# Another order of the rounding steps within a batch row of a conditional MoE and LoRA kernel

## The chip, the cores and the metric

One core of a Trainium2 chip runs the whole kernel. The metric is the device time of one execution in microseconds; lower is better. TensorE (PE) multiplies, VectorE (DVE), ScalarE (ACT) and GpSimd (POOL) do elementwise work, SyncE (SP) issues the DMAs. Each of them has its own queue of instructions, and semaphores tie the queues together.

## The reference

Eight batch rows of `x`, each 512 x 256, go through a mixture of experts with a residual, and then through a linear layer with a LoRA part and a residual. A row has its own two experts of eight, picked by `cond_8`, and one expert shared by all rows.

```python
# layer 0, for each batch row
w, sel = top_k(softmax(cond_8), 2); w = w / w.sum()
mlp(x, g, u, d) = (gelu(x @ g) * (x @ u)) @ d          # g, u: 256 x 1024, d: 1024 x 256
x = x + sum(w[e] * mlp(x, skill_gate[e], skill_up[e], skill_down[e]) for e in sel) \
      + mlp(x, shared_gate, shared_up, shared_down)
# layer 1
out  = einsum('btc,oc->bto', x, W_base) + b_base
h    = einsum('btc,erc->bter', x, As)                  # 8 adapters of rank 16
lora = einsum('bter,eor,be->bto', h, Bs, cond_8)
x = x + out + lora * 2.0
```

## The kernel before

**Numbers.** All matmuls are fp32 in three passes. Every operand is rounded to a short format (ACT, `take_hi`, written "hi") and its remainder is kept too (DVE, `take_lo`: operand minus hi, written "lo"); a product is hi x hi + hi x lo + lo x hi. Rounding and remainder together are called a split. So each weight and each activation passes ACT, then DVE, before TensorE may use it.

**Stages.** First the shared expert is done for all rows (until about 259 us), its result kept in DRAM. Then come the eight batch rows, called row 0 to row 7 here: row 0 is written out, rows 1 to 6 are a loop of three turns with two rows each, row 7 is written out. This change touches only the rows. A row takes some 68 us.

**Steps of a row.** A row has 16 steps, `k` = 0 to 15, one for each 128 of the 1024 hidden columns of its first and then of its second expert. Two steps share a pair of weights: pair 0 to pair 7 of a row, which lie in slot `pair % 4` of `raw` (raw weights, loaded by SP; slots 0 and 1 are called `raw`, 2 and 3 `xbuf`) and of `wide` (the split weights). In step `k` TensorE multiplies gate and up for `k` (into `ring`, 12 matmuls of 512 columns) and then down for step `k - 2` (into `ps_acc`, 6 matmuls). ACT takes the gelu, DVE multiplies gelu, up and the expert's weight (L1711), ACT rounds the product (`inner_hi`), DVE takes its remainder (`inner_lo`).

**Seven-product pairs.** Pairs 3, 5 and 7 (`SEVEN`) do both steps at once, at `k` = 6, 10 and 14, in seven block products instead of eight: 42 matmuls of 256 columns. They need sums of blocks of the weights (POOL makes them, `sums_of_weights`; ACT and DVE split them, `split_sums_w`) and sums of blocks of x (`split_sums_x`). The results come out of PSUM by two ACT copies (L1292) and DVE additions: `ex_v` at L1660, for which the seventh product waits, then L1662, L1669, L1671. Behind the 42 come the downs of the two steps before, into `ps_acc`.

**What else lies in a row.** Step 1: DVE adds up the previous row's result (`layer1_sum`, L1629) and it is split. Step 3: TensorE runs the previous row's second layer (`layer1`, 12 matmuls, `ps_acc`). Step 4: ACT adds the bias (`add_bias`, L1253), DVE transposes the output in blocks (`turn_output`, L1639). Step 8: LoRA's B, scaled by the row's `cond`, is split (`BW_STEP`, L1358 and L1726). Step 9: TensorE folds A and B (`fold`) and the next row's x is split (`X_STEP - 1`). Step 12: DVE adds the folded weights to W, `w_eff` (L1746); step 13: that is split. Row 0 alone has constants at step 4 (`CONST_STEP`): TensorE transposes W and B, ACT and DVE split A, DVE copies and adds the identity (`layer1_constants`, L1615 to L1620).

**What sets the order.** Nothing but the order in which each engine's part is written: ACT and DVE have the same loop over `k`, and two tables say at which step they split which pair and which sums:

```python
SPLIT_AT = {0: 2, 2: 3, 5: 4, 6: 5, 9: 6, 10: 7, 13: 8, 14: 9}
SUMS_AT = {2 * pr - 2: n_s for n_s, pr in enumerate(SEVEN)}
```

Pairs 8 and 9 are the next row's pairs 0 and 1, and the sums stand at steps 4, 8 and 12. A split of a pair waits until SP's load has landed and until TensorE is done with the old weights in that slot of `wide`; DVE's half waits for ACT's. TensorE asks for pair `p` at step `2p` (`weights_ready`), and SP loads a slot again when the pair in it is split.

Of the kernel before, what the change touches and what calls it, by code (L numbers as in the profile page):

```python
# [35 lines left out]
def cond_resid_kernel(nc, x, cond, skill_gate, skill_up, skill_down, shared_gate, shared_up,  # L36
# [15 lines left out]
    L1_STEP = 3  # L52
    CONST_STEP = 4
    BW_STEP = 8
# [3 lines left out]
    X_STEP = 10  # L58
# [6 lines left out]
    with ExitStack() as ctx:  # L65
# [317 lines left out]
        SPLIT_AT = {0: 2, 2: 3, 5: 4, 6: 5, 9: 6, 10: 7, 13: 8, 14: 9}  # L383
        SUMS_AT = {2 * pr - 2: n_s for n_s, pr in enumerate(SEVEN)}
# [675 lines left out]
        def _(act):  # L1060
# [251 lines left out]
            def row(b, par, first, last):  # L1312
                def split_pair(k):
                    pr = SPLIT_AT[k]
                    if pr >= 2 * PAIRS:
                        if not last:
                            split_routed(b + 1, 0, pr - 2 * PAIRS, down_done, b * K + 2 * pr - 6)
                    elif pr >= PAIRS:
                        split_routed(b, 1, pr - PAIRS, down_done, b * K + 2 * pr - 6)
                    elif first:  # L1320
                        split_routed(b, 0, pr, product_done, products(NU - PAIRS + pr, UP, NP - 1))
                    else:
                        split_routed(b, 0, pr, down_done, b * K + 2 * pr - 6)

                for k in range(K):
                    if k // 2 in SEVEN:
                        if k % 2 == 0:
                            n_s = SEVEN.index(k // 2)
                            ex_copy_out(b, n_s, first)
                            split_pair(k)  # L1330
# [12 lines left out]

                    if k == W_EFF_STEP + 1:
                        act.wait_ge(w_eff_done, b + 1)
                        take_hi(w_eff_s[0], w_eff[:]).then_inc(w_eff_hi, 1)
                    if k == (4 if first else 3):
                        split_sums_x(b, first)
                    if k in SUMS_AT:
                        split_sums_w(b, SUMS_AT[k])  # L1350
                    if k in SPLIT_AT:
                        split_pair(k)
# [13 lines left out]
                    if k == 1 and not first:  # L1366
                        layer1_hi(b - 1)
                    if k == L1_STEP + 1 and not first:
# [6 lines left out]
                    if k == X_STEP - 1 and not last:  # L1375
# [15 lines left out]
        def _(dve):  # L1391
# [292 lines left out]
            def row(b, par, first, last):  # L1684
                def split_pair(k):
                    pr = SPLIT_AT[k]
# [5 lines left out]
                for k in range(K):  # L1692
                    s = k // IC
                    if k // 2 in SEVEN:
                        if k % 2 == 0:
                            ex_seven(b, par, k, SEVEN.index(k // 2))
                            split_pair(k)
# [22 lines left out]
                    if k in SUMS_AT:  # L1720
                        split_sums_w(b, SUMS_AT[k])
                    if k in SPLIT_AT:
                        split_pair(k)
# [10 lines left out]
                    if first and k == 1:  # L1734
                        acc1_to_stage(Q - 1)
                    if k == L1_STEP + 1 and not first:
# [3 lines left out]
                    if k == X_STEP - 1 and not last:  # L1740
# [68 lines left out]
```

## Time and profile before

| | us |
|---|---|
| median of 3 runs | 804.69 (803.77 to 805.49) |
| profiled execution | 805.0 |
| its span, first to last instruction | 803.2 |
| granted TensorE clock in it | 0.999 |

| engine | busy share of the span |
|---|---|
| PE | 99% |
| DVE | 84% |
| ACT | 59% |
| POOL | 34% |

Read it so: times are counted from the first instruction. A line like `378.56 0.88 PE L733 MATMUL ps_ring<-... x6` is six matmuls written at line 733 that begin at 378.56 and of which the last ends 0.88 us later; a matmul's end is modelled, so the next begins before it. `[0.47 <-DVE post L1660]` means that the engine stood idle for 0.47 us and that a DVE instruction of line 1660, which writes `post`, ended it. `inner`, `ex_v` and most working tiles are parts of one buffer, `post`; sums and x are in `stage` and `xc`.

### The profile page before, as it was taken

The page shows a single profiled execution, that of the slowest core. Times are in us where ns is not written, and L with a number is a line of the kernel's source. Part 1 is how long each engine was busy: PE and PEld are TensorE (multiplying, and loading weights), DVE is VectorE, ACT ScalarE, POOL GpSimd, SP SyncE. Part 2 cuts the span into 40 slices and gives each one's busy share as a digit, 9 for nine tenths or more (in the row PEclk, how much of TensorE's full clock was granted, in tenths as well). Part 3 has the DMA queues.
Part 4 walks back from the last instruction along what each step waited for, and adds up shares of the span by engine and source line. Part 5 has one row for each costly group of instructions (what it writes and reads, how often), then busy time and mean ns, then how long its engine had stood idle before and what let it go on. Part 6 is the DMA issues. An engine that isn't in the chain of part 4 may idle for free.

```text
span 803.2 us, 13016 instructions
## 1 busy us (share of the span) xinstructions
PE 795.5 (99%) x4014; PEld 679.7 (85%) x4014; DVE 670.9 (84%) x874; ACT 472.1 (59%) x715; POOL 271.9 (34%) x266
## 2 busy tenths in 40 slices
PE   9999999999999999999999999999999999999998
PEld 7888888888888888889888888888888888888887
DVE  3886987987876799799979879987987997999786
ACT  5574564564654565566556556656665665665563
POOL 1440321321110562443246044333404614423420
PEclk9999999999999999999999999999999999999999
DMA  6340520303213432353443335335244423634200
GB/s 198 86 119 11 147 79 12 120 1 97 100 40 80 159 117 79 105 144 107 137 122 97 104 101 158 111 104 131 89 125 138 122 79 104 161 97 135 66 1 28
DMA packets 120143, 80.56 MB, mean 100 GB/s; under 512 B 62481, under 2 KB 115473, under 8 KB 120081
## 3 DMA queue, kind: packets, MB, share of 16 engines
q1 hardware_dynamic: 120080, 79.88, 33.8%
q8 instruction: 21, 0.34, 0.2%
q14 instruction: 42, 0.34, 0.1%
HBM read 67.28 MB, written 12.58 MB: 99 GB/s over the span
## 4 chain that ended last, share of the span: by engine, by line
PE 91%; DVE 4%; issue 2%; POOL 1%; ACT 1%; DMA 0%; DVEq 0%; POOLq 0%; ACTq 0%
PE ps_ring L733 57%; PE ps_acc L733 33%; DVE inner_lo L1395 1%; DVE wide L1395 1%; DVE xc L1395 1%; PE ps_ring L853 1%; DVE post L1711 0%; DMA sh_scratch<-stage 0%; DVE post L1660 0%; PE ps_acc L941 0%; PE ps_acc L847 0%; ACT xc L1062 0%; DVE post L1651 0%; POOL post L692 0%; ACT wide L1062 0%
## 5 line engine op out<-in xcount | busy, mean ns | idle before, releaser
L733 PE MATMUL ps_ring<-xc,wide 128*128 128x512 f32 (+1 forms) x2076 | 454.9, 367 | 1.8 <-DVE post L1660 1.8
L733 PEld LDWEIGHTS ps_ring<-xc,wide 128*128 128x128 f32 x2076 | 366.1, 188 | 68.6 <-DVE post L1660 2.7
L1062 ACT CAST inner_hi<-post 128x512 fp32r<-128x512 f32 x192 | 117.8, 621 | 131.6 <-DVE post L1711 57.8
L733 PE MATMUL ps_acc<-inner_hi,wide 128*128 128x512 f32 x504 | 172.0, 390 | 0.0
L1395 DVE TENSOR_TENSOR inner_lo<-post,inner_hi 128x512 fp32r<-128x512 f32 x192 | 163.6, 866 | 6.7 <-ACT inner_hi L1062 5.7
L1065 ACT ACTIVATE post<-ps_ring 128x512 f32<-128x512 f32 (+1 forms) x132 | 73.4, 559 | 92.2 <-PE ps_ring L733 86.3
L733 PEld LDWEIGHTS ps_acc<-inner_hi,wide 128*128 128x128 f32 x504 | 94.7, 188 | 19.2
L692 POOL TENSOR_TENSOR post<-post 128x256 f32<-128x256 f32 x48 | 34.5, 740 | 214.6 <-DVE post L1662 214.6
L733 PE MATMUL ps_acc<-inner_lo,wide 128*128 128x512 f32 x252 | 98.3, 390 | 0.0
L1711 DVE SCALAR_TENSOR_TENSOR post<-post,coef_now,ps_ring 128x512 f32<-128x512 f32 x80 | 59.5, 744 | 42.1 <-PE ps_ring L733 39.0
L733 PE MATMUL ps_acc<-inner_hi,sh_dn 128*128 128x512 f32 x256 | 83.8, 389 | 0.0
L733 PE MATMUL ps_ring<-xc 128*128 128x256 f32 x576 | 77.2, 283 | 0.5 <-DVE post L1711 0.5
L621 POOL TENSOR_TENSOR post<-post 128x512 f32<-128x512 f32 x24 | 31.1, 1294 | 135.5 <-DVE post L1447 135.5
L1395 DVE TENSOR_TENSOR wide<-raw,wide 128x1536 fp32r<-128x1536 f32 (+3 forms) x38 | 62.5, 1644 | 15.8 <-ACT wide L1062 15.8
L1065 ACT ACTIVATE post<-post 128x256 f32<-128x256 f32 (+1 forms) x84 | 46.4, 569 | 49.5 <-DVE post L1669 33.6
L733 PEld LDWEIGHTS ps_ring<-xc 128*128 128x128 f32 x576 | 72.6, 192 | 0.7 <-DVE post L1711 0.7
L1395 DVE TENSOR_TENSOR wide<-xbuf,wide 128x1536 fp32r<-128x1536 f32 x32 | 57.4, 1793 | 0.0
L733 PEld LDWEIGHTS ps_acc<-inner_hi,sh_dn 128*128 128x128 f32 x256 | 48.0, 188 | 9.9
L1062 ACT CAST wide<-raw 128x1536 fp32r<-128x1536 f32 (+3 forms) x40 | 52.2, 1306 | 4.8 <-DMA raw<-_L_cond_shared_gate_dram 3.7
L733 PEld LDWEIGHTS ps_acc<-inner_lo,wide 128*128 128x128 f32 x252 | 47.4, 188 | 9.0
L733 PE MATMUL ps_acc<-inner_lo,sh_dn 128*128 128x512 f32 x128 | 49.8, 389 | 0.0
L1395 DVE TENSOR_TENSOR xc<-stage,xc 128x1024 fp32r<-128x1024 f32 (+1 forms) x41 | 47.6, 1166 | 0.0
(122 smaller groups left out, 847.1 us busy)
## 6 DMA issues: line engine op xcount, KB each, us to landing
raw<-n_L_cond_skill_gate_dram SPq DMA_DIRECT2D x32, 256.0 KB, 2.9
raw<-in_L_cond_skill_up_dram SPq DMA_DIRECT2D x32, 256.0 KB, 3.4
raw<-n_L_cond_skill_down_dram SPq DMA_DIRECT2D x32, 256.0 KB, 3.7
xbuf<-n_L_cond_skill_gate_dram SPq DMA_DIRECT2D x32, 256.0 KB, 2.9
xbuf<-in_L_cond_skill_up_dram SPq DMA_DIRECT2D x32, 256.0 KB, 3.4
xbuf<-n_L_cond_skill_down_dram SPq DMA_DIRECT2D x32, 256.0 KB, 4.1
xt_scratch<-xbuf SPq DMA_DIRECT2D x8, 512.0 KB, 3.1
sh_scratch<-stage SPq DMA_DIRECT2D x8, 512.0 KB, 2.7
```

Source lines behind the costliest of these rows:

```text
L621: G.tensor_tensor((g_t if part == GATE else i_t)[3], v57, u1, ALU.add).then_inc(c22_done, 1)
L692: last = G.tensor_tensor(ex_v[:, half], ex_v[:, half], ex_u1[:, half], ALU.add)
L733: last = pe.matmul(dst, left_[a], right_[b], start=start and n == 0, stop=stop and n == len(PASSES) - 1, skip_group_check=adds)
L853: pe.transpose(ring[3][:, 0:P], ident[:], ident[:])
L1062: return nc.scalar.copy(dst, src)
L1065: return nc.scalar.activation(dst, src, ACT.Gelu_apprx_tanh)
L1395: return V.tensor_tensor(dst, src, hi.bitcast(F32), ALU.subtract)
L1711: V.scalar_tensor_tensor(out=inner[k % 2], in0=gelu[k % 2], scalar=coef_now[:, par, s:s + 1], in1=ring[2 + k % 2][:], op0=ALU.mult, op1=AL ...
```

## The change

Both ACT and DVE get new tables and a few moved calls. Row 0 keeps the old places of its splits (`SPLIT_FIRST`), the other rows get `SPLIT_LATER`:

- Step 14 splits nothing any more. The next row's pair 1 is split by that row itself, at step 0. Pair 2 goes from step 0 to 2, pair 3 from step 2 to the end of step 3, behind `inner_hi` and `inner_lo`, and with it the first sums of the weights, from step 4. In row 0 these stay.
- At step 13, on ACT, the sums, the pair's rounding (the next row's pair 0) now stand ahead of the rounding of `w_eff`. DVE's order there is the old one.
- LoRA's B is split at step 5 instead of 8, the next row's x at the end of step 8 instead of 9, row 0's constants at step 3 instead of 4 on PE, ACT and DVE.

```diff
-    CONST_STEP = 4
-    BW_STEP = 8
+    CONST_STEP = 3
+    BW_STEP = 5
-    X_STEP = 10
+    X_STEP = 8
-        SPLIT_AT = {0: 2, 2: 3, 5: 4, 6: 5, 9: 6, 10: 7, 13: 8, 14: 9}
-        SUMS_AT = {2 * pr - 2: n_s for n_s, pr in enumerate(SEVEN)}
+        SPLIT_FIRST = {0: 2, 2: 3, 5: 4, 6: 5, 9: 6, 10: 7, 13: 8}
+        SPLIT_LATER = {0: 1, 2: 2, 5: 4, 6: 5, 9: 6, 10: 7, 13: 8}
+        SUMS_FIRST = {4: 0, 8: 1, 12: 2}
+        SUMS_LATER = {8: 1, 12: 2}
...
+                    if k == (4 if first else 3):
+                        split_sums_x(b, first)
+                    if k in sums_at:
+                        split_sums_w(b, sums_at[k])
+                    if k in split_at:
+                        split_pair(split_at[k])
                     if k == W_EFF_STEP + 1:
                         act.wait_ge(w_eff_done, b + 1)
                         take_hi(w_eff_s[0], w_eff[:]).then_inc(w_eff_hi, 1)
-                    if k == (4 if first else 3):
-                        split_sums_x(b, first)
-                    if k in SUMS_AT:
-                        split_sums_w(b, SUMS_AT[k])
-                    if k in SPLIT_AT:
-                        split_pair(k)
...
+                    if k == L1_STEP and not first:
+                        split_pair(SEVEN[0])
+                        split_sums_w(b, 0)
...
-                    if k == X_STEP - 1 and not last:
+                    if k == X_STEP and not last:
```

The last two pieces stand in ACT's loop and in DVE's. Line numbers of the changed program are 3 to 15 higher than those of the old one: L1711 is L1723 there, L1660 is L1669, L1395 is L1404 and ACT's L1062 is L1065.

ACT, from the gelu of step 13 to the seven-product pair at step 14, row 0 (the loop's rows are the same with register instructions between). Before:

```order
L1065 ACTIVATE post<-ps_ring 128x512
L1062 CAST xc<-w_eff 128x512
L1062 CAST wide<-raw 128x1536
L1062 CAST inner_hi<-post 128x512
L1292 COPY post<-ps_ring 128x512 x2
L1062 CAST wide<-raw 128x1536
L1065 ACTIVATE post<-ps_ring 128x256
```

And now:

```order
L1068 ACTIVATE post<-ps_ring 128x512
L1065 CAST wide<-raw 128x1536
L1065 CAST xc<-w_eff 128x512
L1065 CAST inner_hi<-post 128x512
L1295 COPY post<-ps_ring 128x512 x2
L1068 ACTIVATE post<-ps_ring 128x256
L1068 ACTIVATE post<-post 128x256
```

The pair in `raw` has gone ahead of `w_eff`, and the second pair behind the copies is gone.

DVE in the loop, from the multiplication of step 3 to the transpose of step 4. `xc<-stage` is the lo of a sum (of x, then of weights), `wide<-xbuf` the lo of pair 3. Before:

```order
L1711 SCALAR_TENSOR_TENSOR post<-post,coef_now,ps_ring 128x512
L1395 TENSOR_TENSOR xc<-stage,xc 128x1024
L1729 REGISTER_ALU
L1395 TENSOR_TENSOR inner_lo<-post,inner_hi 128x512
L1699 REGISTER_ALU
L1711 SCALAR_TENSOR_TENSOR post<-post,coef_now,ps_ring 128x512
L1646 ISA
L1395 TENSOR_TENSOR xc<-stage,xc 128x1024
L1729 REGISTER_ALU
L1395 TENSOR_TENSOR inner_lo<-post,inner_hi 128x512
L1637 REGISTER_ALU
L1639 STREAM_TRANSPOSE stage<-post 128x1024
```

And now (the transpose is the next computing row):

```order
L1723 SCALAR_TENSOR_TENSOR post<-post,coef_now,ps_ring 128x512
L1404 TENSOR_TENSOR xc<-stage,xc 128x1024
L1741 REGISTER_ALU
L1404 TENSOR_TENSOR inner_lo<-post,inner_hi 128x512
L1437 REGISTER_ALU
L1404 TENSOR_TENSOR wide<-xbuf,wide 128x1536
L1655 ISA
L1404 TENSOR_TENSOR xc<-stage,xc 128x1024
L1711 REGISTER_ALU
L1723 SCALAR_TENSOR_TENSOR post<-post,coef_now,ps_ring 128x512
L1741 REGISTER_ALU
L1404 TENSOR_TENSOR inner_lo<-post,inner_hi 128x512
```

Pair 3 and the sums of the weights stand between `inner_lo` of step 3 and the multiplication of step 4; step 4 has lost its sums.

DVE in row 0, from the multiplication of step 4 to `inner_lo` of step 5. Before:

```order
L1711 SCALAR_TENSOR_TENSOR post<-post,coef_now,ps_ring 128x512
L1395 TENSOR_TENSOR xc<-stage,xc 128x1024 x2
L1395 TENSOR_TENSOR inner_lo<-post,inner_hi 128x512
L1395 TENSOR_TENSOR xc<-post,xc 128x256
L1615 COPY b_t<-ps_acc 128x256
L1616 COPY w_id<-ps_acc 128x512
L1620 TENSOR_TENSOR w_id<-w_id,ident 128x128 x2
L1711 SCALAR_TENSOR_TENSOR post<-post,coef_now,ps_ring 128x512
L1395 TENSOR_TENSOR wide<-raw,wide 128x1536
L1395 TENSOR_TENSOR inner_lo<-post,inner_hi 128x512
```

And now, from behind `inner_lo` of step 3:

```order
L1404 TENSOR_TENSOR xc<-post,xc 128x256
L1624 COPY b_t<-ps_acc 128x256
L1625 COPY w_id<-ps_acc 128x512
L1629 TENSOR_TENSOR w_id<-w_id,ident 128x128 x2
L1723 SCALAR_TENSOR_TENSOR post<-post,coef_now,ps_ring 128x512
L1404 TENSOR_TENSOR xc<-stage,xc 128x1024 x2
L1404 TENSOR_TENSOR inner_lo<-post,inner_hi 128x512
L1723 SCALAR_TENSOR_TENSOR post<-post,coef_now,ps_ring 128x512
L1404 TENSOR_TENSOR wide<-raw,wide 128x1536
L1738 SCALAR_TENSOR_TENSOR xc<-b_t,coef_now,xc 128x256
L1404 TENSOR_TENSOR inner_lo<-post,inner_hi 128x512
```

The five constant rows (`xc<-post`, `b_t`, `w_id`) stand ahead of step 4's multiplication, and B's lo (L1738) has come in behind pair 4.

## Rows read from the trace of the kernel before

**Rows 1.** The page's part 1: busy us (share of the span) xinstructions of each engine.

```profile
PE 795.5 (99%) x4014; PEld 679.7 (85%) x4014; DVE 670.9 (84%) x874; ACT 472.1 (59%) x715; POOL 271.9 (34%) x266
```

**Rows 2.** Waits of TensorE: who waited for whom, us in total, times, longest.

```profile
PE ps_ring L733 <- DVE post L1660: 1.8, 4, 0.7
PE ps_ring L733 <- DVE post L1711: 0.5, 1, 0.5
```

**Rows 3.** The chain that ended last, in order of time: start us, us, what.

```profile
346.12 5.03 PE ps_ring L733 x42
...
515.28 5.18 PE ps_ring L733 x42
...
718.46 5.23 PE ps_ring L733 x42
```

**Rows 4.** Timeline of PE: start, us, engine, line, op, out<-in, shapes, xcount [idle before].

```profile
293.43 0.88 PE L733 MATMUL ps_ring<-xc,wide 128*128 128x256 f32 x6
...
299.10 0.40 PE L733 MATMUL ps_acc<-inner_hi,wide 128*128 128x512 f32 x1
...
378.56 0.88 PE L733 MATMUL ps_ring<-xc,wide 128*128 128x256 f32 x6
...
383.50 0.98 PE L733 MATMUL ps_ring<-xc,wide 128*128 128x256 f32 x6 [0.47 <-DVE post L1660]
...
384.31 0.40 PE L733 MATMUL ps_acc<-inner_hi,wide 128*128 128x512 f32 x1
```

**Rows 5.** Timeline of ACT, row 1, step 13.

```profile
377.78 0.62 ACT L1062 CAST xc<-w_eff 128x512 fp32r<-128x512 f32 x1 [1.14 <-DVE w_eff L1746]
378.31 1.47 ACT L1062 CAST wide<-raw 128x1536 fp32r<-128x1536 f32 x1
```

**Rows 6.** Timeline of DVE, row 1, step 13 and the seven behind it.

```profile
377.67 0.73 DVE L1711 SCALAR_TENSOR_TENSOR post<-post,coef_now,ps_ring 128x512 f32<-128x512 f32 x1
379.81 1.76 DVE L1395 TENSOR_TENSOR wide<-raw,wide 128x1536 fp32r<-128x1536 f32 x1 [1.41 <-ACT wide L1062]
...
382.76 0.68 DVE L1660 TENSOR_TENSOR post<-ps_ring,post 128x512 f32<-128x512 f32 x1
```

**Rows 7.** Timeline of DVE, row 1, steps 0 and 3 to 6.

```profile
322.63 1.75 DVE L1395 TENSOR_TENSOR wide<-xbuf,wide 128x1536 fp32r<-128x1536 f32 x1
...
335.92 1.22 DVE L1395 TENSOR_TENSOR inner_lo<-post,inner_hi 128x512 fp32r<-128x512 f32 x1
340.79 0.75 DVE L1711 SCALAR_TENSOR_TENSOR post<-post,coef_now,ps_ring 128x512 f32<-128x512 f32 x1 [3.65 <-PE ps_ring L733]
341.45 1.22 DVE L1395 TENSOR_TENSOR xc<-stage,xc 128x1024 fp32r<-128x1024 f32 x1
342.59 0.68 DVE L1395 TENSOR_TENSOR inner_lo<-post,inner_hi 128x512 fp32r<-128x512 f32 x1
343.57 1.25 DVE L1639 STREAM_TRANSPOSE stage<-post 128x1024 f32<-128x1024 f32 x1 [0.30 <-ACT post L1253]
...
348.41 0.69 DVE L1660 TENSOR_TENSOR post<-ps_ring,post 128x512 f32<-128x512 f32 x1 [0.53 <-PE ps_ring L733]
```

**Rows 8.** Timeline of PE, row 1, the first matmuls of step 2.

```profile
326.92 2.88 PE L733 MATMUL ps_ring<-xc,wide 128*128 128x512 f32 x12
```

**Rows 9.** Timeline of POOL, row 1, the four additions of x to the shared part.

```profile
334.87 4.26 POOL L708 TENSOR_TENSOR post<-post 128x256 f32<-128x256 f32 x4
```

**Rows 10.** Timeline of DVE, row 0, steps 4 to 10.

```profile
274.98 0.96 DVE L1395 TENSOR_TENSOR xc<-post,xc 128x256 fp32r<-128x256 f32 x1
...
277.32 0.74 DVE L1711 SCALAR_TENSOR_TENSOR post<-post,coef_now,ps_ring 128x512 f32<-128x512 f32 x1
...
280.25 0.68 DVE L1660 TENSOR_TENSOR post<-ps_ring,post 128x512 f32<-128x512 f32 x1
...
291.45 0.96 DVE L1726 SCALAR_TENSOR_TENSOR xc<-b_t,coef_now,xc 128x256 fp32r<-128x256 f32 x1
...
297.55 0.68 DVE L1660 TENSOR_TENSOR post<-ps_ring,post 128x512 f32<-128x512 f32 x1
```

## What the change does to the time

> **What bounds the kernel now.** I read the page first: TensorE is busy 795.5 of 803.2 us [rows 1], and its granted clock is 0.999 of full speed, so this is a kernel that waits for matmuls, and only an instant at which TensorE itself stands still can be won or lost. Then the waits of TensorE alone: apart from the start of the kernel they are five, four of them for the DVE addition at L1660 (1.8 us) and one for the DVE multiplication at L1711 (0.5 us) [rows 2]. All five lie in the seven-product pairs. Then the chain of work that ended last, in order of time: a seven-product pair (42 matmuls) that waits for nothing takes 5.03 us, and the same 42 matmuls at the end of rows 3, 4 and 5 take 5.18 to 5.19 (the first of the three stands there) and of row 6 5.23 [rows 3]; the difference is a wait too short to be listed as one. Last the timeline of TensorE around the long ones, from the first of the 42 matmuls to the first matmul behind them: 293.43 to 299.10 is 5.67 us, 378.56 to 384.31 is 5.75 us [rows 4].
>
> The timeline also tells how idle time turns into loss. The seventh product at 383.50 has 0.47 us of idle before it, yet the pair lost 5.75 - 5.03 = 0.72 [rows 4]. The other 0.25 is hidden in the modelled end of a matmul and in the restart of the pipe. So a listed wait costs its idle time plus 0.25 us. The nine losses:
>
> - row 0, first seven (the L1711 wait): 0.5 + 0.25 = 0.75 [rows 2].
> - row 0, second seven: 5.67 - 5.03 = 0.64 [rows 4].
> - last seven of row 1: 0.72 [rows 4].
> - last seven of rows 0 and 2: the four L1660 waits add to 1.8 [rows 2], row 1 has 0.47 of it and the second seven of row 0 at most 0.64 - 0.25 = 0.39; 0.94 to 1.33 is left for these two, with twice 0.25 a loss of 1.44 to 1.83. I take the middle, 1.6.
> - last seven of rows 3 to 6: 3 x 0.15 + 0.20 = 0.65 [rows 3].
>
> Sum 0.75 + 0.64 + 0.72 + 1.6 + 0.65 = **4.4 us**, give or take 0.2. It is also the most that the change can give in the eight rows; the rest of them runs at the matmuls' own pace.
>
> **Why the last seven of a row waits.** Its seventh product needs `ex_v`, added on DVE at L1660, 4.32 us after the first product has started (six products of 5.03/7 = 0.72). In row 1 that is 378.56 + 4.32 = 382.88; the addition runs from 382.76 to 383.44 [rows 6], 0.56 too late. Before it DVE stands idle 1.41 us for ACT's rounding of the next row's pair 0 [rows 6]. ACT did that rounding at 378.31, because it first waited 1.14 us for DVE's `w_eff` and rounded that [rows 5]. Everything DVE does between is back to back.
>
> **The change part by part.**
>
> Step 13, pair 0 of the next row ahead of `w_eff`. ACT's previous operation, the gelu of step 13, ends 1.14 us before 377.78, at 376.64 [rows 5]. The 1.47 us rounding then runs 376.6 to 378.1 instead of 378.31 to 379.8, `w_eff` follows (0.62 us, to 378.7; its input has been there since 377.78), then `inner_hi` and the two copies. DVE finishes its multiplication at 378.40 and needs no wait: the remainder of the pair starts at 378.40 instead of 379.81, 1.41 us earlier, and L1660 could start at 382.76 - 1.41 = 381.35. It also needs the third product (378.56 + 3 x 0.72 + 0.15 = 380.9) and the second of ACT's copies, which starts behind the second product at 380.2 and, as an ACT operation of 512 columns (0.62 us), ends near 380.8. So it ends at 382.0, 0.85 us before it is needed. The loss was 0.56; all seven losses at the ends of rows go: **-2.97 us** (0.72 + 1.6 + 0.65). The last row has no next row, no split at step 13 and no loss there now, which fits.
>
> Step 14 to step 0, pair 1. DVE's remainder of this pair stood between the last seven and the first multiplication; at step 0 it takes the place that pair 2 had, with the same instruction (1.75 us, 322.63 to 324.38, in row 1) [rows 7]. TensorE asks for pair 1 at step 2, at 326.92 [rows 8]: **0**, with a cover of 2.5 us. SP loads slot 1 again only behind this, some 2.4 us later than before; ACT asks for that load at step 6, over 20 us on, and nothing that stands behind it in SP's queue starts sooner than DVE's sum at step 1 allows.
>
> Steps 2 and 3, pairs 2 and 3. Pair 2 now stands at step 2, where pair 3 stood, and TensorE asks for it two steps later: 0. Pair 3 and the weights' sums move behind `inner_lo` of step 3, into the 3.65 us in which DVE waits for TensorE to finish the previous row's second layer [rows 7]. `inner_lo` starts at 335.92 and takes 1.22 us, and an operation on DVE starts some 0.08 before the recorded end of the one ahead (341.45 + 1.22 against 342.59), so the next can start at 337.06. Then 1.67 for the pair (1.75 less 0.08) and 1.14 for the sums (341.45 to 342.59 now) end at **339.9**; the multiplication of step 4 is due at 340.79. TensorE asks for pair 3 at the next seven, 346.12 in the chain [rows 3]: 0. In this hole POOL adds `x` to the shared part, 334.87 to 339.13 [rows 9]. Beside it `inner_lo` took 1.22 us where it takes 0.68 at 342.59 [rows 7], 0.54 more. So the two moved operations cost between 2.8 us and 2.8 + 2 x 0.54 = 3.9 us of DVE. At the upper end DVE is free at 340.95, and step 4 is 0.2 us late. I take the upper end, since the nearest row, `inner_lo` in that very hole, is disturbed; 0.2 us are covered further on (rival 3), so **0** on the path.
>
> Step 8 to 5, LoRA's B. In loop rows DVE waits 0.53 us for TensorE before L1660 of the first seven (348.41) [rows 7]. The operation is 0.96 us, pace 0.89 [rows 10], of which 0.53 is covered: L1660 moves by 0.36 to end at 349.46. The wait ends with the third product; the seventh starts three products after the third has ended, less the 0.15 us in which they overlap: 348.41 + 2.16 - 0.15 = 350.4, or 350.3 with the hand-over. Cost 0, cover 0.8 us.
>
> Step 9 to 8, x. It stays ahead of the second seven, behind one multiplication less: 0 there. That step 8 lost B is worth 0.89 us to L1660 of the second seven. Row 0 is the one that needs it: L1660 ended at 298.23 [rows 10], needed at 293.43 + 4.32 = 297.75, 0.48 late; now 0.4 early. **-0.64 us**.
>
> Row 0, constants from step 4 to 3. From 274.98 to 277.32 DVE does A's remainder and four constant operations, 2.34 us, right before the multiplication on which the first seven waits [rows 10]. Now they stand behind step 3, where DVE waited for TensorE; TensorE's own transposes only change places. The multiplication of step 5 starts at about 275.5 (the gap before step 4's takes all but half a microsecond of the 2.34), needed at 277.4 (TensorE goes on behind it at 278.1 now and has lost 0.7 there; so this seven began at 277.4 - 2 x 0.72 = 275.98): the L1711 wait goes. But B's 0.89 us now stand between it and L1660: 280.25 - 1.8 + 0.9 = 279.35, end 280.05, needed at 275.98 + 4.32 = 280.30. Only 0.25 us of cover, and POOL is busy here. Between -0.75 and -0.25 (a lateness of 0.25 with 0.25 for the restart); I take **-0.7**.
>
> Sum: -2.97 - 0.64 - 0.7 = **-4.3 us**. Against the profiled run's 805.0 (its span 803.2 and 1.8 around it) this is 800.7; the median of the three runs shown is 0.3 lower, 804.69, so I say **800.4**.
>
> **A rule that speaks against it.** DVE's `inner_lo` took 1.22 us while POOL was adding and 0.68 us when it was not [rows 7, 9]. The Trainium skill, SBUF — State Buffer, section Who interferes with whom, says that a DVE instruction with two SBUF inputs and a GpSimd instruction that reads SBUF exclude each other for a whole instruction. By that rule, with which the trace agrees in kind, each operation moved into step 3 may have to wait out a whole POOL addition. What that would do here is priced, from rows, in rival 3.
>
> **The rivals.**
>
> 1. Row 0 keeps part of its losses (the thin 0.25 us above fails, or the constants disturb step 4). For it: this is the only place with a cover under 0.4 us, under a busy POOL. Price 0.3 to 1.2 us back: 800.7 to 801.6. Chance 0.17.
>
> 2. The swap at step 13 does not do what it says: another input of L1660 (the copies behind `inner_hi`, the registers that ACT computes between) is late too. Against it: every one of them is done by 380.9 in the sum. Half to all of the 2.97 us would stay: 801.9 to 803.4. Chance 0.08.
>
> 3. Slower: the hole of step 3 is overfilled. DVE's step 4 goes late, then `add_bias` on ACT, the transpose at 343.57 [rows 7] and step 5, since that chain reaches 344.82 just when TensorE's step 5 is ready; so lateness at step 4 passes on entirely, and B's 0.36 us come on top. It decides from 0.8 us: DVE free after 341.6 instead of 339.9 to 341.0. With POOL's additions of 4.26/4 = 1.07 us each [rows 9] waited out in full twice, DVE is free at 342.0, 1.2 late, 0.4 beyond the cover; with a restart of 0.1 to 0.25 that is 0.5 to 0.65 us in each of seven rows, 3.5 to 4.5 us, and the gain is eaten: 804. For a loss of more than 0.2% it must be 342.3 or later: 806.4. Against it: the disturbed row adds 0.54 us, not 1.07. Chance of within 0.2% of before 0.04, of slower 0.03.
>
> **How the numbers follow.** Forecast 800.4 with 0.68 (799.8 to 800.8); rival 1 0.17; rival 2 0.08; rival 3 0.07. The range is to hold the time 8 times in 10: the forecast and rival 1 and the near part of rival 2, 799.5 to 802.0. The lower end is the full 4.4 to 4.6 and the half microsecond by which the runs' median may be off (runs shown: 803.77 to 805.49). A measurement of this kernel tells about 0.2%, 1.6 us, from no change: faster means below 803.1. Forecast, rival 1 and nearly all of rival 2 are there: 0.92; the same 0.05; slower 0.03.
>
> **What would show it.** In the changed kernel's chain every seven-product pair from row 1 on reads 5.03 or 5.04; TensorE's waits for the L1660 operation are gone, and DVE's for ACT's `wide` at step 13 too. DVE's 3.65 us before step 4 shrink under 1 us and the multiplication still starts in TensorE's time. In the first seven of row 0 the addition ends within 0.3 us of its need, on either side. I am wrong if a loop row shows a wait in its first seven, or if step 2 of a row waits for pair 1.

## The result and the profile after

| | before | after |
|---|---|---|
| median | 804.87 (6 runs, 803.77 to 805.49) | 800.72 (6 runs, 800.03 to 801.29) |
| profiled execution | 805.0 | 800.03 |
| its span | 803.2 | 798.2 |
| granted clock in it | 0.999 | 0.999 |

The ratio of the medians is 0.9949 (0.9939 to 0.9959): faster by 4.15 us, 0.5%. Forecast were 800.4 us and 4.3 us. The two profiled spans differ by 5.0 us. From the first matmul of row 0's first seven to that of row 7's last seven there are 510.09 us before and 505.81 after, 4.28 less. I call this time the stretch. The other 0.7 us lie ahead of the rows, where nothing is changed: row 0's first seven starts at 275.98 and at 275.31, and in the runs below it is anything from 275.1 to 277.4.

First the totals of the changed kernel, to be held against [rows 1] (columns as there). TensorE is busy 2.6 us less with the same 4014 matmuls; since a matmul's end is modelled, a stalled matmul counts in part as busy.

```profile
PE 792.9 (99%) x4014; PEld 678.4 (85%) x4014; DVE 676.6 (85%) x874; ACT 470.1 (59%) x715; POOL 290.5 (36%) x266
```

The waits of TensorE after (us in total, times, longest). These two are all, both from the start of the kernel; the five of [rows 2] are gone.

```profile
PE ps_ring L856 <- POOL ident L593: 1.5, 1, 1.5
PE ps_ring L754 <- ACT xc L1065: 0.3, 1, 0.3
```

The chain that ended last (start, us, what), for [rows 3]: the sevens of row 0, row 1 and the last one of row 7. All read 5.03 or 5.04, but for row 0's second.

```profile
275.47 5.03 PE ps_ring L736 x42
...
292.12 5.19 PE ps_ring L736 x42
...
308.22 5.03 PE ps_ring L736 x42
...
343.20 5.03 PE ps_ring L736 x42
...
359.86 5.04 PE ps_ring L736 x42
...
375.80 5.03 PE ps_ring L736 x42
...
781.28 5.03 PE ps_ring L736 x42
```

Step 13 of row 1 on ACT, for [rows 5] (start, us, engine, line, op, out<-in, shapes, xcount, idle before). The pair's rounding follows the gelu at once, `w_eff` comes behind it.

```profile
373.12 0.60 ACT L1068 ACTIVATE post<-ps_ring 128x512 f32<-128x512 f32 x1 [0.56 <-PE ps_ring L736]
373.61 1.47 ACT L1065 CAST wide<-raw 128x1536 fp32r<-128x1536 f32 x1
374.98 0.62 ACT L1065 CAST xc<-w_eff 128x512 fp32r<-128x512 f32 x1
```

The same place on DVE, for [rows 6]. The remainder of the pair starts with no wait; `ex_v` (L1669 now) ends at 378.83. This seven started at 375.64, so it is needed at 375.64 + 4.32 = 379.96: 1.1 us early, where it was 0.56 late.

```profile
374.55 0.75 DVE L1723 SCALAR_TENSOR_TENSOR post<-post,coef_now,ps_ring 128x512 f32<-128x512 f32 x1 [0.39 <-PE ps_ring L736]
375.21 1.75 DVE L1404 TENSOR_TENSOR wide<-raw,wide 128x1536 fp32r<-128x1536 f32 x1
...
378.15 0.68 DVE L1669 TENSOR_TENSOR post<-ps_ring,post 128x512 f32<-128x512 f32 x1
```

Steps 3 to 5 of row 1 on DVE, for [rows 7]. The 3.65 us of waiting before step 4 are filled completely. Pair 3 took 2.29 us and the sums 1.75.

```profile
334.14 2.29 DVE L1404 TENSOR_TENSOR wide<-xbuf,wide 128x1536 fp32r<-128x1536 f32 x1
336.36 1.75 DVE L1404 TENSOR_TENSOR xc<-stage,xc 128x1024 fp32r<-128x1024 f32 x1
338.04 0.73 DVE L1723 SCALAR_TENSOR_TENSOR post<-post,coef_now,ps_ring 128x512 f32<-128x512 f32 x1
...
344.28 0.48 DVE L1738 SCALAR_TENSOR_TENSOR xc<-b_t,coef_now,xc 128x256 fp32r<-128x256 f32 x1
```

POOL's four additions of x in row 1, for [rows 9]: 6.77 us instead of 4.26. POOL paid more for the two moved operations than DVE did.

```profile
331.94 6.77 POOL L711 TENSOR_TENSOR post<-post 128x256 f32<-128x256 f32 x4
```

**All sevens in one table.** For each I took the time from its first matmul to the first matmul behind its 42, less 5.03 (the loss), and in brackets when `ex_v` ended against 4.32 us after its start (plus is late). "Rows 1 to 6" gives a range where they differ.

| kernel | row 0: first, second, last | rows 1 to 6: first, second, last | losses, us |
|---|---|---|---|
| before | 0.78, 0.64 (+0.49), 0.97 | 0, 0 (-0.46 to -1.02), row 1 0.72, row 2 0.68, others 0.15 to 0.20 | 4.46 |
| after | 0 (-0.31), 0.16 (0.00), 0 (-0.63) | 0, 0, 0 (-1.17, -1.17, -1.12) | 0.16 |

They fell by 4.30, and the stretch by 4.28. So between these two executions the whole effect is in these 24 places, and what is left is one loss. The losses count only what is lost inside the 24 sevens; the stretch counts what is lost between them too, and where the two differ below, the stretch decides.

### The profile page after: what moved, and what is told of

Read it like the earlier page. It is cut to its first block, busy times and chain, and to the rows that moved or that the text cites. A ratio compares the mean times of both kernels' runs of the same rounds, so it can differ in the third digit from the quotient of the medians.

```text
span 798.2 us, 13016 instructions
## 1 busy us (share of the span) xinstructions
PE 792.9 (99%) x4014; PEld 678.4 (85%) x4014; DVE 676.6 (85%) x874; ACT 470.1 (59%) x715; POOL 290.5 (36%) x266
## 4 chain that ended last, share of the span: by engine, by line
PE 99%; DMA 1%; DVE 0%; ACT 0%; SPq 0%; DVEq 0%; issue 0%
PE ps_ring L736 62%; PE ps_acc L736 36%; DMA raw<-_L_cond_shared_gate_dram 1%; PE ps_acc L944 0%; PE ps_acc L964 0%; PE ps_ring L754 0%; DVE stage L1798 0%; PE ps_ring L758 0%; PE ps_ring L762 0%; PE ps_acc L850 0%; PE ps_ring L964 0%; ACT xc L1065 0%; PE ps_acc L990 0%; ACT wide L1065 0%; SPq L456 0%
## 5 line engine op out<-in xcount | busy, mean ns | idle before, releaser
L1065 ACT CAST inner_hi<-post 128x512 fp32r<-128x512 f32 x192 | 117.9, 621 | 140.8 <-DVE post L1723 67.6
L1404 DVE TENSOR_TENSOR inner_lo<-post,inner_hi 128x512 fp32r<-128x512 f32 x192 | 162.1, 858 | 12.2 <-ACT inner_hi L1065 11.8
L695 POOL TENSOR_TENSOR post<-post 128x256 f32<-128x256 f32 x48 | 34.5, 741 | 187.7 <-DVE post L1671 187.7
L1723 DVE SCALAR_TENSOR_TENSOR post<-post,coef_now,ps_ring 128x512 f32<-128x512 f32 x80 | 59.4, 742 | 30.7 <-PE ps_ring L736 25.4
L1404 DVE TENSOR_TENSOR wide<-raw,wide 128x1536 fp32r<-128x1536 f32 (+3 forms) x38 | 62.5, 1644 | 7.7 <-ACT wide L1065 7.7
L1404 DVE TENSOR_TENSOR wide<-xbuf,wide 128x1536 fp32r<-128x1536 f32 x32 | 60.3, 1885 | 0.0
L1065 ACT CAST wide<-raw 128x1536 fp32r<-128x1536 f32 (+3 forms) x40 | 52.2, 1306 | 4.9 <-DMA raw<-_L_cond_shared_gate_dram 3.6
L711 POOL TENSOR_TENSOR post<-post 128x256 f32<-128x256 f32 x32 | 51.6, 1641 | 0.0
L1404 DVE TENSOR_TENSOR xc<-stage,xc 128x1024 fp32r<-128x1024 f32 (+1 forms) x41 | 51.3, 1258 | 0.0
```

What stands on the lines that cost most here:

```text
L695: last = G.tensor_tensor(ex_v[:, half], ex_v[:, half], ex_u1[:, half], ALU.add)
L711: done = G.tensor_tensor(base[:, part], base[:, part], xf[:, part], ALU.add)
L1065: return nc.scalar.copy(dst, src)
L1404: return V.tensor_tensor(dst, src, hi.bitcast(F32), ALU.subtract)
L1723: V.scalar_tensor_tensor(out=inner[k % 2], in0=gelu[k % 2], scalar=coef_now[:, par, s:s + 1], in1=ring[2 + k % 2][:], op0=ALU.mult, op1=AL ...
```

## The experiments

**The theories.** Theory A, the prediction's: each loss has a cause of its own, so the parts of the change add up. Theory B: what DVE is late with in one seven it is late with in the next, because it works back to back between them, so the parts overlap. Theory C, for rows 1 and 2, which lose 0.7 where rows 3 to 5 lose 0.15 with the same code: the order in which DVE's and POOL's operations happen to meet. The kernels that were timed in several rounds have their interval; the others are single executions, read by their traces.

**Only the swap** (before, with the pair ahead of `w_eff` on ACT).

```diff
+                    if k == (4 if first else 3):
+                        split_sums_x(b, first)
...
+                    if k in SPLIT_AT:
+                        split_pair(k)
                     if k == W_EFF_STEP + 1:
                         act.wait_ge(w_eff_done, b + 1)
                         take_hi(w_eff_s[0], w_eff[:]).then_inc(w_eff_hi, 1)
-                    if k == (4 if first else 3):
...
```

> The kernel before with one edit: at step 13 ACT rounds the next row's pair 0 ahead of w_eff. Theory A (each loss has its own cause): the losses at the ends of rows 0 to 6 go, -3.0 us, and the two losses of row 0's first and second seven stay at about 0.8 and 0.64; 801.9 us by the median, last sevens 5.03 each in the chain. Theory B (the last seven is late mostly because DVE arrives late from the second seven): the swap gives about as much here, since it shortens the same chain by 1.4 us, so this run alone does not tell the two apart; it tells both from 'the swap does nothing' (804.9).

Measured 801.70 us (801.11 to 802.13) beside 805.30 of before on that chip, ratio 0.995 (0.9933 to 0.9966). All the last sevens lose nothing (0.94 to 1.12 early in the loop), where they lost 3.0 before. Row 0 keeps 0.76 in the first seven and 0.17 in the second, but that is no gain: TensorE waits at the fold just ahead of the second one, and from the end of the first seven to the start of the second there are 12.15 us instead of 11.63. These 0.52 and the 0.17 come to as much as the 0.64 of before.

```profile
PE ps_ring L733 <- DVE post L1711: 0.5, 1, 0.5
...
PE ps_acc L733 <- DVE xc L1726: 0.3, 1, 0.3
```

So two roundings that change places on ACT give 3.6 us by the medians and 2.96 of the 4.28 by the stretch (507.13 instead of 510.09).

**Everything but the swap** (the changed kernel, `w_eff` ahead again).

> The changed kernel with that one edit undone: w_eff is rounded first again, all other moves stay. Theory A: the seven last losses come back in full, 3.0 us, 803.7 us, with waits for the ex_v addition in rows 0, 1 and 2 of 0.4 to 0.7 us. Theory B: DVE now reaches step 12 earlier since B has left step 8, so rows 0 to 2 fall to what rows 3 to 6 had before, 0.15 to 0.2 each, 1.1 to 1.4 us in all, 801.9 us, and no wait is long enough to be listed.

Measured 802.42 us (801.49 to 802.87), ratio 0.996 (0.9946 to 0.9974). By the losses the swap is worth only 1.64 here (1.80 left instead of 0.16): 1.04 in row 0, 0.28 in row 1, 0.06 in each of the others, where by Theory A it should be the 3 of above. Yet the wait that the swap removes is there, on DVE at step 13 of rows 0 and 1:

```profile
309.44 1.76 DVE L1404 TENSOR_TENSOR wide<-raw,wide 128x1536 fp32r<-128x1536 f32 x1 [1.41 <-ACT wide L1065]
...
377.31 1.76 DVE L1404 TENSOR_TENSOR wide<-raw,wide 128x1536 fp32r<-128x1536 f32 x1 [1.15 <-ACT wide L1065]
```

The table of lateness tells why. In every kernel without the swap the `ex_v` of a loop row's last seven is later than that of its second seven, each against its own need, by the same amount:

| kernel, row | second seven | last seven | difference |
|---|---|---|---|
| before, 1 | -0.46 | +0.57 | 1.03 |
| before, 3 to 5 | -1.02 | 0.00 | 1.02 |
| everything but the swap, 1 | -0.89 | +0.13 | 1.02 |
| everything but the swap, 2 | -1.17 | -0.09 | 1.08 |

The swap removes this step of 1.02 (with it -1.17 becomes -1.12). The other moves shift the second seven, and with it the last. By the stretch the swap alone gives 2.96 us, the other moves alone 2.66 (507.43), both together 4.28; behind the other moves the swap gives 1.61. This is Theory B for rows 1 to 6; Theory A holds in the last seven of row 0, where the swap is worth about 1 us in both settings. The recorded text gave Theory B 1.1 to 1.4 us of losses and 801.9 us; they are 1.80 and 802.42, because it took row 0's last seven for one of those that shrink, and it did not.

**The moves of pairs alone** (the changed kernel, swap undone, and B, x and the constants back).

```diff
-    CONST_STEP = 3
-    BW_STEP = 5
+    CONST_STEP = 4
+    BW_STEP = 8
-    X_STEP = 8
+    X_STEP = 9
```

> The kernel before with only the pairs moved: the next row's pair 1 from step 14 to step 0, pairs 2 and 3 to steps 2 and 3, the first sums to step 3. w_eff first, B at 8, x at the end of 9, constants at 4 as before. Both theories: no loss of TensorE touches these steps, so 0, 804.9 us (within 0.3), and all nine losses are still there. If the pair behind the copies of step 14 was part of the last losses, they shrink. In step 3 DVE should be free 0.1 to 0.3 us after TensorE's step 4 is ready.

Measured 804.29 us (803.49 to 805.15), ratio 0.9988 (0.9978 to 0.9997). Expected was no difference; the medians show 1.0 us, with an interval that just leaves out 1. In rows 1 to 6 every last seven loses 0.16 to 0.21, no 0.7 among them. That is 1.0 us less than in the trace of before, but before itself shows 0.14 to 0.16 in five of these rows in other executions (Theory C, below, with what the moves may have to do with it). Row 0's last seven keeps its loss, 1.03, and its second has 0.17 with the same 12.15 us ahead of it as in "only the swap".

**Only B at step 5.**

```diff
-    BW_STEP = 8
+    BW_STEP = 5
```

> The kernel before with LoRA's B split at step 5 instead of 8, nothing else. Both theories: the second seven of row 0 loses its 0.64, and the first seven of row 0, whose DVE chain is full of constants, loses 0.4 to 0.9 more. Theory A: the ends of rows stay as they are; net 0 to +0.3, 804.9 to 805.2 us. Theory B: the ends of rows 0, 1 and 2 fall from 1.0, 0.7 and 0.7 to about 0.2 each, -1.8 us; 803.1 to 803.4 us.

Measured 804.11 us (802.99 to 804.96), ratio 0.9983 (0.9974 to 0.9993). Row 0's first seven gets worse, 1.18 instead of 0.78, its second better, 0.37 instead of 0.64; rows 1 to 6 keep 0.06 to 0.42 in the last, and row 0's last keeps 1.06. So neither recorded expectation is met: the ends of the loop's rows shrink, as Theory B has it, the end of row 0 does not, and the time lies between the two forecasts. The stretch is 509.21 us; before's, in its three executions, are 509.30 to 510.09. On DVE in row 0 the five constants still stand ahead of the multiplication of step 5, and B's remainder now stands behind it, ahead of `ex_v`:

```profile
276.69 0.74 DVE L1711 SCALAR_TENSOR_TENSOR post<-post,coef_now,ps_ring 128x512 f32<-128x512 f32 x1
277.35 1.75 DVE L1395 TENSOR_TENSOR wide<-raw,wide 128x1536 fp32r<-128x1536 f32 x1
279.01 0.48 DVE L1726 SCALAR_TENSOR_TENSOR xc<-b_t,coef_now,xc 128x256 fp32r<-128x256 f32 x1
...
280.01 0.69 DVE L1660 TENSOR_TENSOR post<-ps_ring,post 128x512 f32<-128x512 f32 x1
```

B costs its 0.40 us in full there. This also gives its true price: the recorded 0.96 (pace 0.89) of [rows 10] was beside POOL; undisturbed it is 0.48 (pace 0.40).

**Before twice more**, no edit, for Theory C.

> The kernel before, unchanged, profiled once more. Theory A (fixed causes): the same nine losses as in the first profile, 0.78, 0.64, 0.97 in row 0, 0.72 and 0.68 at the ends of rows 1 and 2, 0.15 to 0.20 at the ends of rows 3 to 6, 4.5 us in all. Theory C (lock order: rows with the same instructions differ because DVE's operations with two SBUF inputs and POOL's additions meet in one order or the other, worth about 0.5 us each time): the rows with 0.7 and those with 0.15 are others than before, row 0's second seven is 0.64 or 0.17, and the sum lies anywhere from 2.9 to 6.

> The kernel before once more. Theory A: as in the first profile, 4.5 us of losses. Theory C: again another set of rows with 0.7 and 0.15; the first profile's seven and this one's agree in row 0's first seven (0.8) alone.

Measured 804.40 and 804.41 us, both with a span of 802.6 against 803.2. The losses sum to 3.63 and 3.83 instead of 4.46. Row 0 is the same to 0.03 (0.76, 0.64, 0.97 in both). Row 1's last seven loses 0.50 and 0.70 instead of 0.72, row 2's 0.14 and 0.15 instead of 0.68. The same code, another loss: rows 1 and 2 have no fixed price. Row 0's second seven, for which Theory C allowed 0.17 too, is not among the places that vary here.

The trace shows where the executions part, in row 2, ahead of the second seven. DVE runs the same sequence in both, 0.05 us apart. POOL waits there until the last of the eight DMAs that store the previous row's output has landed (`out_dram<-stage`), and only then makes the sums of x for the next row. In the profiled execution of before this comes 1.0 us later than in the second trace (the second sevens begin at 430.91 and 430.86). So POOL's last sum falls on DVE's `inner_lo`, which takes 1.22 instead of 0.68. Before, POOL, then DVE:

```profile
426.38 1.73 POOL L660 TENSOR_TENSOR stage<-post 128x256 f32<-128x256 f32 x1 [2.88 <-DMA out_dram<-stage]
...
430.22 2.25 POOL L665 TENSOR_TENSOR stage<-post,stage 128x256 f32<-128x256 f32 x1
...
431.79 1.22 DVE L1395 TENSOR_TENSOR inner_lo<-post,inner_hi 128x512 fp32r<-128x512 f32 x1
```

The second trace of the same kernel:

```profile
425.36 0.91 POOL L660 TENSOR_TENSOR stage<-post 128x256 f32<-128x256 f32 x1 [1.91 <-DMA out_dram<-stage]
...
429.02 1.07 POOL L665 TENSOR_TENSOR stage<-post,stage 128x256 f32<-128x256 f32 x1
...
431.74 0.68 DVE L1395 TENSOR_TENSOR inner_lo<-post,inner_hi 128x512 fp32r<-128x512 f32 x1
```

The three executions of before have 18 such rows in the loop, and the start of this first sum sorts them all:

| first sum starts, ahead of the second seven | rows | `ex_v` of the second seven | loss of the last seven |
|---|---|---|---|
| 4.48 to 4.56 us | 3 | -0.48 to -0.46 | 0.68 to 0.72 |
| 4.89 us | 1 | -0.68 | 0.50 |
| 5.18 to 5.58 us | 14 | -1.02 to -0.97 | 0.14 to 0.20 |

The difference is then carried to the last seven, past a second meeting. In before DVE's two multiplications by the expert's weight (L1651) run in one piece and slowly, while POOL starts its sums (L678) a hundredth of a microsecond ahead of them. DVE and POOL:

```profile
436.91 2.15 DVE L1651 SCALAR_TENSOR_TENSOR post<-post,coef_now 128x256 f32<-128x256 f32 x2
...
436.90 0.74 POOL L678 TENSOR_TENSOR stage<-xbuf 128x256 f32<-128x256 f32 x1
```

In the second trace POOL is 0.44 us ahead, and DVE is done at 438.47 instead of 439.06, although it waited 0.18 for ACT in between:

```profile
436.74 0.58 DVE L1651 SCALAR_TENSOR_TENSOR post<-post,coef_now 128x256 f32<-128x256 f32 x1
437.50 0.97 DVE L1651 SCALAR_TENSOR_TENSOR post<-post,coef_now 128x512 f32<-128x512 f32 x1 [0.18 <-ACT post L1065]
...
436.30 0.74 POOL L678 TENSOR_TENSOR stage<-xbuf 128x256 f32<-128x256 f32 x1
```

Before was within 0.0 to 0.6 us of its need in every last seven of rows 1 to 6, so half a microsecond more or less was a loss more or less. In the changed kernel all of rows 1 to 6 have at least 1.1 us of cover, and all six read alike. The moved pairs may have a share in it. The first sum starts less than 4.9 us ahead of the second seven in 10 of 36 loop rows in the six executions with the pairs in their old places, and in 3 of 36 in the six with them moved (the two with fillers, below, left out). What would bring the store forward I did not look for, so this is a count and not a shown cause.

**The constants at step 4**, and **B at step 8**, each one number changed back in the changed kernel (`CONST_STEP`, `BW_STEP`).

> The changed kernel with row 0's constants back at step 4. All theories: the first seven of row 0 loses again what it lost before, 0.75, plus B's 0.4 to 0.9 which now stands in the same chain (1.2 as in the kernel with B alone moved); rows 1 to 7 lose nothing. 1.2 to 1.6 us of losses in all, a time of 801.9 to 802.3.

> The changed kernel with LoRA's B back at step 8. Row 0's second seven loses 0.2 to 0.9 (x and B both ahead of it), its first seven nothing, the addition ending 0.7 to 1.2 early instead of 0.3. Theory A: the loop rows lose nothing, the addition of the last seven ends 0.85 early. Theory C: the same losses, but the addition of the loop's second and last seven is early by two different amounts, 0.5 apart, from row to row, where the changed kernel has -1.17 and -1.12 in each.

Measured 801.63 us with losses of 1.49, and 800.28 us with losses of 0.11. With the constants at 4, row 0's first seven loses 1.18, as in "only B at step 5", and its second 0.31; by the stretch (507.15) moving them is worth 1.34 us, in both sevens together. With B at 8, DVE waits 0.52 us for TensorE again in row 1's first seven (L1669, at 345.71), row 0's first seven is 0.71 early instead of 0.31, and the second sevens of the loop rows have 0.47 of cover where they had 1.17. Row 0's second seven loses 0.11 with B back at 8, where the recorded text expected 0.2 to 0.9, and 0.16 with B moved. In this kernel B's move gains nothing; it takes cover from the first seven and, in the loop, gives some to the second.

**The swap and the constants, nothing else** (the first edit and `CONST_STEP = 3`).

> The kernel before with two edits alone: ACT rounds the next row's pair 0 ahead of w_eff at step 13, and row 0's constants go to step 3. The split pairs, B and x stay where they were. If these two carry the change: the seven last sevens and row 0's first lose nothing, row 0's second loses 0 to 0.64 (by the lock order), 800.7 to 801.3 us, no different from the changed kernel. If moving pairs, B or x is needed for the cover: losses of 0.15 and more at the ends of rows, 802 us or more.

Measured 801.49 us (801.07 to 802.13), ratio 0.9951 (0.9934 to 0.9968). The losses sum to 0.12. Its profiled execution reached the first seven of row 0 only at 277.41, after a wait of 1.9 us near 37 us, in the shared expert, that no other trace has at this length, and from there to the last seven took 505.78 us, as the changed kernel does (505.81). So these two edits carry the whole gain in the eight rows, and by the stretch they add up: 2.96 for the swap, 1.34 for the constants. The overlap found above is between the swap and the others (pairs, B, x). The median is 0.8 above the changed kernel's, which was timed in another comparison; the ratios to before are the same (0.9951 and 0.9949). On its own chip `x_late_row0`, below, is 1.1 us faster. Whether that is the wait in the shared expert or something the trace doesn't show is open.

**Filling the hole of step 3 further**, for rival 3: one or two sums over `raw[3]` that nobody reads, on DVE between pair 3 and the weights' sums, in rows 1 to 7 (added work; 1.21 us recorded, pace 1.12 each).

```diff
                     if k == L1_STEP and not first:
                         split_pair(SEVEN[0])
+                        V.tensor_reduce(waste[:, 0:1], raw[3][:, 0:1024], AX_X, ALU.add)
                         split_sums_w(b, 0)
```

> The changed kernel with one added DVE operation (a sum over 1024 columns of the raw weights, about 1.1 us) in step 3 of rows 1 to 7, ahead of the remainder of the sums. The multiplication of step 4 starts 1.1 us later, 1.3 behind TensorE. If the cover is the 0.8 us of the prediction (decides at 0.8, price the excess and a restart): the first seven of each row loses 0.5 to 0.75, 3.5 to 5 us. If the cover is what the changed kernel's trace shows, 1.17 us before the need and 0.13 us of idle in front of the addition, B's remainder having cost 0.4 and not 0.9: no loss or under 0.2 per row, 800.0 to 801.5 us.

> The same with two such operations, 2.2 us. Cover 0.8: each first seven loses 1.6 to 1.9 us, 11 to 13 us in seven rows. Cover 1.3 to 1.5: 0.9 to 1.2 us each, 6.5 to 8.5 us. A time of 807 to 809 us would be slower than the kernel before: the point at which the filled hole of step 3 costs more than the change gives.

Measured 800.51 and 803.55 us. One filler costs nothing: the first sevens still have 0.70 to 0.74 of cover (row 7's 0.51). With two they lose 0.43 to 0.46 in each of rows 1 to 6 and 0.77 in row 7, 3.4 us in all, where the lowest recorded expectation was 6.5 us and 807 us. Steps 3 and 4 of row 1 with two fillers, on DVE:

```profile
334.26 2.30 DVE L1405 TENSOR_TENSOR wide<-xbuf,wide 128x1536 fp32r<-128x1536 f32 x1
336.48 1.21 DVE L1751 TENSOR_REDUCE waste<-xbuf 128x1 f32<-128x1024 f32 x1
337.61 1.20 DVE L1752 TENSOR_REDUCE waste<-xbuf 128x1 f32<-128x1024 f32 x1
338.73 1.21 DVE L1405 TENSOR_TENSOR xc<-stage,xc 128x1024 fp32r<-128x1024 f32 x1
339.87 0.73 DVE L1724 SCALAR_TENSOR_TENSOR post<-post,coef_now,ps_ring 128x512 f32<-128x512 f32 x1
```

The 2.24 us of filler made step 4 only 1.72 later against the first seven (it starts 3.28 ahead of it instead of 5.00), since the sums fell back from 1.75 to 1.21 us: by then POOL was done. With one filler it is 0.71 later. Row 1's `ex_v` is 0.31 late and 0.70 early in these two, so in the changed kernel DVE has 1.72 - 0.31 = 1.41 or 0.71 + 0.70 = 1.41 us to spare for it; the 1.17 of the table is less because `ex_v` waits for the third product there. So the place is real and a loss does appear, but from 1.4 us beyond the changed kernel's state, not from the 0.6 that the prediction left (0.8 less the 0.2 that step 4 is late anyway).

**x one step later in row 0 alone.**

```diff
-                    if k == X_STEP and not last:
+                    if k == (9 if first else X_STEP) and not last:
```

> The changed kernel, with x split at the end of step 9 in row 0 alone. In the changed kernel x's remainder takes 1.76 us there because POOL is adding, and the addition of row 0's second seven ends just when it is needed, a loss of 0.16. At step 9 POOL is through: 1.21 us, the addition 0.5 early, all 24 seven-product pairs at 5.03; 0.16 us less than the changed kernel, 800.6 us, which timing cannot tell from it, but the chain of waits can.

Measured 800.38 us (800.35 to 800.46), ratio 0.9939 (0.9923 to 0.9956), losses 0.00. This takes away the one loss that the change leaves. Row 0 in the changed kernel, then in this one, on DVE: at step 8 the remainder of x lies beside a POOL addition and takes 1.76 us, behind the second seven's first product it takes 1.21. (With B back at step 8 it took 1.21 at step 8 as well: B's going is what brought it beside POOL.)

```profile
290.99 1.76 DVE L1404 TENSOR_TENSOR xc<-post,xc 128x1024 fp32r<-128x1024 f32 x1
...
295.60 0.68 DVE L1669 TENSOR_TENSOR post<-ps_ring,post 128x512 f32<-128x512 f32 x1
```

```profile
294.45 1.21 DVE L1404 TENSOR_TENSOR xc<-post,xc 128x1024 fp32r<-128x1024 f32 x1
295.58 0.68 DVE L1669 TENSOR_TENSOR post<-ps_ring,post 128x512 f32<-128x512 f32 x1
```

Both `ex_v` stand at the same time, but this seven began 0.52 us later (the first seven too: 275.99 against 275.47 in the chain). The edit is worth 0.16 us at most, less than the two medians can tell apart (800.38 and 800.72).

## Why the prediction was right, and where its steps were off

- **What bounds the kernel: right.** All of the change shows in the 24 sevens, 4.28 us by the two profiled executions. The sum of the losses ahead was put at 4.4, measured 4.46. That a listed wait costs 0.25 beyond its idle time held where it was long enough to read: without the swap, row 0's last seven has 0.8 of it listed and lost 1.04.
- **The swap, predicted -2.97: right in mechanism and cover was better, 1.12 instead of 0.85.** But it treated 0.72 and the 0.68 of row 2 as fixed properties of those rows. They are a meeting of DVE and POOL that depends on when a store lands, 0.50 to 0.72 in row 1 and 0.14 to 0.68 in row 2 over three executions. The size is right for the execution that was summed; for the median of before it is up to 0.8 too much. And it is not independent of the other moves: by the stretch it is worth 2.96 us alone and 1.61 behind them. The sum came out because the other moves were given nothing in these sevens; had each part been priced by itself and added (2.96 by the swap, 2.66 by the moves), it would have been 5.6, more than there is to lose.
- **Row 0's second seven, predicted -0.64 with 0.4 us of cover, by B's leaving step 8: the size nearly right, the cause wrong.** It gained 0.48, and it gains 0.53 with B back at step 8 and 0.52 with the swap and the constants alone, where B and x stay where they were. What cured it is the constants' move: DVE works nearly without a pause from the first seven's `ex_v` to the second's, 17.30 us before and 17.34 with B at 8, so the second is about as late as the first was, and the constants made the first earlier. B's leaving was priced at 0.89 and shortened this time only to 16.97, because it brought the remainder of x beside POOL, 1.76 instead of 1.21; and B at step 5 gave 0.40 back ahead of the first `ex_v`. So the step "x stays ahead of the second seven: 0" failed too, and in the sum nothing was left of B's gain: `ex_v` ended exactly when needed, which still costs 0.16. `x_late_row0` takes that away. The two terms for row 0 together, 0.64 + 0.7 = 1.34, are what the constants give by themselves; that this sum came out is luck.
- **Row 0's first seven, predicted -0.7 with a cover of 0.25: measured -0.78 with 0.31.** Errors cancel in the cover: B was priced at 0.89 and took 0.40; the sums of x and weights took 3.44 us together instead of the 3.11 that lay in the sum, and the constants pushed step 4's multiplication by 0.67 instead of 0.54.
- **The hole of step 3: right, at its upper end.** Both moved operations took 0.54 more beside POOL (2.29 and 1.75 instead of 1.75 and 1.21), as the nearest row said. Step 4's multiplication ran 0.17 late, predicted 0 to 0.2. The first seven has 1.4 us to spare instead of 0.6; 0.49 of the difference is B, which cost 0.40 instead of 0.89.
- **Rival 3 had the right place and too high a price.** Its point of decision is 0.8 us further off than it said, and overfilled by 2.24 us the kernel was at 803.55, still not slower than before. Its assumption, that an operation waits out whole POOL additions, did not come about. The Trainium skill, SBUF — State Buffer, section Who interferes with whom, has a DVE instruction with two SBUF inputs contend with a GpSimd instruction that reads SBUF, by an exclusive lock. DVE paid 0.54 us per operation here, beside POOL additions of 1.07. POOL paid more: its four additions went from 4.26 to 6.77 us.
- **What would show it: as said.** Sevens of 5.03 and 5.04 from row 1 on, the waits gone, the idle time before step 4 below 1 us (0), row 0's first seven within 0.3 of its need (0.31). The miss, row 0's second seven at 5.19, was outside that list.

What is open: the effect of the moved pairs on the loop rows, of which there is only a count, and the 0.8 us between the medians of swap-and-constants and of the changed kernel.

## What to carry to other kernels

When the engine that bounds a kernel waits in few places, list each place with how early or late its input came, not only the wait: two edits that each bring the missing half microsecond to the same place do not add up, and one of them may do. On an engine that waits for another's output, look for what the other did while it waited for the first; here one rounding ahead of another on ACT was 2.96 of 4.28 us. Here a cover of under half a microsecond beside a second elementwise engine was lost or won by when that engine was released, so before a loss is called a property of a row, look at a second execution. And when two edits come together, take one back: B's move had the credit for what the constants did.

## What the runs showed of the hardware that was not expected

- A DVE `TENSOR_TENSOR` with two SBUF inputs that loses time to POOL mostly loses a fixed step, not a share: 0.54 us for 512, 1024 and 1536 columns (0.68 to 1.22, 1.21 to 1.75, 1.75 to 2.29). Not all of them lose it. Of those that lay wholly beside POOL's work in the rows of the 14 traces, 548 of 576 took 1.2 us at 512 columns; at 1536 columns 84 of 176 took 2.3 and 81 took 1.7 to 1.8; at 1024 columns 121 of 291 took 1.7 to 1.8, 65 took 1.2 and the rest lay between.
- With one SBUF input no such step shows: 604 additions of 512 columns with the other input in PSUM took 0.7 us wholly beside POOL's work, as without it, and the filler (a sum, 1.21 us each) was the same where POOL's additions were running.
- POOL pays more than DVE: four additions of 256 columns 6.77 us instead of 4.26, for two more DVE operations beside them.
- The same program gave losses of 3.63 and 3.83 us in two executions on one chip and 4.46 in a third execution. What differed was when a store of the output landed and released POOL, by up to 1.0 us in one row; the changed kernel's cover of 1.1 us keeps this from TensorE.
